# The experts' end of a four-layer kernel: gathers issued together, slot numbers ahead of other work, shared rows added by VectorE, four result and output buffers

## The chip, the cores and the metric

The kernel runs on one core of a Trainium2 chip. The metric is device time in microseconds (us) from the start to the end of one execution; shorter is better. All tensors are float32. TensorE (PE) has two clock levels, 1.2 and 2.4 GHz; the profile gives the granted one as a share of the higher ("PEclk", 0.50 to 1.00).

## What is computed

Eight sequences of 256 rows with 256 columns pass through four residual layers. Each computes `x = x + layernorm(f(layernorm(x)))`. The first three are a state-space mixer with a gated feed-forward, a low-rank mixture of 8 experts, and causal attention. The fourth, where the change lies, is a mixture of 64 experts. In the reference, cut to what matters:

```python
logits = flat @ router_w.T                      # flat: 2048 x 256
_, topk_idx = top_k(logits + router_bias, 4)
topk_w = softmax(logits) at topk_idx, divided by its sum
tok_table = rows of each expert, at most 32     # 64 x 32
xg = flat[tok_table]
g, u = xg @ gate_w, xg @ up_w                   # 256 -> 64, per expert
y = (silu(g) * u) @ down_w                      # 64 -> 256, per expert
out = scatter_add(y * weight) + shared experts(flat)   # 256 -> 512 -> 256
```

## The kernel before

The 2,048 rows are worked on in four rounds of 512, each with four tiles of 128 rows. A round takes its rows through the first three layers. The router, the shared experts and the table of slots of round r-1 are worked in between the first two layers of round r; those of the last round (`LAST` = 3) come behind it by themselves. Each engine has its own program written out by hand, and the engines wait for each other by semaphores. A `BankPlan` gives each PSUM bank its order of users; a user waits until the one before has been read out.

**The last round's router part.** On PE the order is: turn the first half of the normed rows `xf` (`transposes`), `route(0)` (logits of the first half), `project_o(1)` (the attention's last output projection, second half), `shared_hidden(g, 0)` twice (gate and up products of the shared experts for the first half), turn the second half, `route(1)`, `shared_hidden(g, 1)` twice, `shared_down(0)`, `positions` (a running count that gives each choice its place in its expert), `shared_down(1)`, `add_to_table`. On VectorE (DVE): copies of the logits, `routed_experts` (the top four), `routed_counts` (who chose what, for `positions`), `routed_groups` (first the logits of the chosen, a product over 1,024 columns and a sum; then the group of each expert), `shared_gate` for (0, 1) and (1, 1), `routed_slots` (needs `positions`), `routed_places` (first two small operations that release the exponential on ScalarE through `top_ready`; then a 2,048-column comparison, `oh_place`), and `add_rows`, which adds PE's table to the one in SBUF. `result_rows` makes two index tables out of it: `tidx` (which row of `xn_dram` each of the 2,048 slots takes) and `yidx` (to which row of `y_dram` its result goes).

ScalarE (ACT) copies each half of `shared_down` to `tmp` (`shared_sum`), takes the exponential (`expert_exp`), then goes to its part of the experts. SyncE (SP) stores `tmp` into `sh_dram` (`store_shared`), and then loads for all 16 tiles of the output the shared sum and the residual row (`shx[i][:, 0, :]` and `shx[i][:, 1, :]`, 32 transfers of 128 KB) into buffers that by then are free.

**The experts.** The 64 experts are 16 groups of four, worked in eight pairs `p`. The weights are in SBUF. GpSimd (POOL) issues an indirect DMA for each group: `gather(g)` brings 128 rows from `xn_dram` into one of eight buffers `xg`, `scatter(g)` writes 128 result rows from `yt` to `y_dram`. Its order is gathers 0 to 7, then for each pair two scatters and (for the first four) two gathers, into the buffers of the first eight. PE's order for a pair is `turn` (transposes of the gathered rows, bank XG), `gate_up` (32 instructions into 32-column parts of the array, bank GU), `turn_hidden` (HT) and `down` (16 instructions, two banks YO). `turn(p+1)` and `gate_up(p+1)` are issued before `down(p)`. ACT copies XG and HT to SBUF and takes the silu; DVE multiplies (`gate`) and copies YO to `yt` (`results`), of which there are two pairs: `results(p)` waits until the scatters of pair p-2 have landed (`y_out`).

**The sums.** When all scatters have landed, ACT loads tile after tile the four result rows of each of its 128 rows (`yk`, four buffers of 512 KB, queue of ACT). For each of the 16 tiles PE adds in one bank the shared sum (a product with the identity, L570) and the four rows, each by a diagonal matrix of weights (L575). DVE takes mean and variance from the bank (L716, L718, L719), POOL the power (L655), and DVE, one tile behind (`finish`), scales the bank's rows (L708) and adds the residual (L711) into `ot`. There are two `ot`: `finish(i)` waits until the store of tile i-2 has landed (`stored`). SP stores.

Of the kernel before, what the change touches and what calls it, by code (L numbers as in the profile page):

```python
# [107 lines left out]
def sandwich(nc, A, out):  # L108
    with ExitStack() as ctx:
# [334 lines left out]
        xg = [(xin, hn)[s // 4][:, s % 4, :] for s in range(8)]  # L444
# [5 lines left out]
        yt = [u[:, 2 * i:2 * i + 2, :] for i in range(2)]  # L450
# [5 lines left out]
        acc = [tmp[:, s, :] for s in range(2)]  # L456
        ot = [tmp[:, 2 + s, :] for s in range(2)]
# [14 lines left out]
        xg_in = [sem(f"xg_in{s}") for s in range(8)]  # L472
        e_silu = signal("e_silu", EPAIRS)
        y_out = [sem(f"y_out{s}") for s in range(2)]
# [7 lines left out]
        stored = [sem(f"stored{s}") for s in range(2)]  # L482
        chain2 = signal("dve_chain2", 2 * TOKENS // P)
# [15 lines left out]
        def tail_sync(sp):  # L499
            sp.wait_ge(tidx_ready, 1)  # L500
            sp.wait_ge(x3_out, 16 * ROUNDS + CREDIT)
# [5 lines left out]
            for i in range(TOKENS // P):  # L507
                sp.wait_ge(out_ready.sem, i + 1)
                sp.dma_start(out[i * P:(i + 1) * P, :], ot[i % 2]).then_inc(stored[i % 2], 16)
            for s in range(2):  # L510
                sp.wait_ge(stored[s], 16 * (TOKENS // P // 2) + CREDIT)

        def tail_tensor(pe):
            def turn(p):
                for g in (2 * p, 2 * p + 1):
                    pe.wait_ge(xg_in[g % 8], 16 * (g // 8) + 16)
                pe.wait_ge(*tail.before(("XG", p), 0))
                for i in range(2):
                    for k in range(DC):
                        o = (i * DC + k) * P  # L520
                        mm = pe.transpose(tail[("XG", p)][:, o:o + P], xg[(2 * p + i) % 8][:, k * P:(k + 1) * P],
# [43 lines left out]
            for i in range(TOKENS // P):  # L565
# [3 lines left out]
                pe.wait_ge(shx_in[i // 4], 128)  # L569
                mm = pe.matmul(sums[("SUM", i)][:, 0:D], ident[:, :], shx[i][:, 0, :], start=True, stop=False)  # L570
# [3 lines left out]
                for k in range(TOPK):  # L574
                    mm = pe.matmul(sums[("SUM", i)][:, 0:D], diag[i % 2][:, k, :], yk[s][:, k, :],  # L575
                                   start=False, stop=k == TOPK - 1)
                mm.then_inc(sums.fills(("SUM", i)), 1)

        def tail_scalar(act):
# [33 lines left out]
            for s in range(2):  # L613
                act.wait_ge(y_out[s], 16 * EGROUPS // 2)
# [10 lines left out]
        def tail_pool(pool):  # L625
            def gather(g):
                if g >= 8:
                    pool.wait_ge(*tail.full(("XG", g // 2 - 4), 0))
                pool.indirect_dma_start(
                    out=xg[g % 8], out_offset=None, in_=xn_dram,  # L630
                    in_offset=bass.IndirectOffsetOnAxis(ap=tidx[:, g:g + 1], axis=0)).then_inc(xg_in[g % 8], 16)

            def scatter(g):
# [3 lines left out]
                    in_=yt[g // 2 % 2][:, g % 2, :], in_offset=None, bounds_check=TOKENS * TOPK - 1,  # L637
# [1575 lines left out]
```

## Time and profile before

| what | value |
|---|---|
| median of 3 runs | 1291.43 us (1290.85 to 1294.38) |
| profiled execution | 1297.54 us, its span 1295.5 us |
| busy: PE, DVE, ACT, POOL | 1110.3, 867.8, 499.0, 251.8 us |
| instructions | 19826 |
| mean granted PE clock | 0.939 |
| moved by DMA | 111.75 MB |

The span is the time between the first and the last instruction of the profiled execution. The median is of other executions, and is 6.1 us under the profiled one. Times in the views below count from the span's start; the part that the change touches begins at about 1149 us.

### The profile page before, as it was taken

What the parts mean: (1) busy time and instruction counts of PE and PEld (TensorE: products, weight loads), DVE (VectorE), ACT (ScalarE), POOL (GpSimd) and SP (SyncE); (2) the same over time, 40 slices, a digit from 0 to 9 for tenths busy, and PEclk for the clock granted to TensorE, in tenths of its full rate; (3) what the DMA queues carried; (4) which work ended last, traced back from release to release, by engine and by line L of the source; (5) the groups of instructions that cost most, each with busy time, mean ns of one, the idle gap of its engine ahead of it and who ended that gap; (6) DMA issues with size and microseconds to landing.
All of it is one profiled execution on the core that took longest, in us unless ns stands there. A gap on an engine that the chain in (4) does not pass through costs nothing.

```text
span 1295.5 us, 19826 instructions
## 1 busy us (share of the span) xinstructions
PE 1110.3 (86%) x7192; PEld 672.5 (52%) x7192; DVE 867.8 (67%) x1848; ACT 499.0 (39%) x1076; POOL 251.8 (19%) x522
## 2 busy tenths in 40 slices
PE   3999896888998997888998997888998997886667
PEld 1444554554445675554445674554445675465345
DVE  5899526669997545669996636769997546565126
ACT  2766411236665202246665102236664111221133
POOL 3222001132221000222221000222221000222432
PEclk9999998899999997899999997899999997897679
DMA  5888100004431000004331000004348030035345
GB/s 177 284 266 282 36 1 16 1 2 133 120 116 59 1 8 26 2 2 146 121 120 41 1 17 17 1 5 155 122 123 216 4 94 21 2 81 167 118 162 186
DMA packets 72673, 111.75 MB, mean 86 GB/s; under 512 B 5896, under 2 KB 62608, under 8 KB 71682
## 3 DMA queue, kind: packets, MB, share of 16 engines
q1 hardware_dynamic: 68738, 98.51, 24.4%
q10 hardware_dynamic: 2304, 8.39, 2.0%
q0 software_dynamic: 1536, 3.60, 0.9%
q8 instruction: 57, 0.93, 0.3%
q14 instruction: 38, 0.31, 0.1%
HBM read 91.81 MB, written 19.27 MB: 86 GB/s over the span
## 4 chain that ended last, share of the span: by engine, by line
PE 61%; DVE 20%; issue 7%; ACT 6%; DMA 2%; another core or an unknown queue 1%; POOL 1%; DVEq 0%; SPq 0%; POOLq 0%; ACTq 0%
PE bank L883 22%; DVE hf L1651 5%; PE bank L948 4%; PE bank L1124 4%; PE bank L1165 3%; PE bank L1032 3%; PE bank L1048 2%; DVE nmax L2041 2%; PE bank L962 2%; PE bank L1211 2%; DVE u L1871 2%; PE bank L1208 2%; PE bank L896 2%; DMA out_dram<-tmp 2%
## 5 line engine op out<-in xcount | busy, mean ns | idle before, releaser
L883 PE MATMUL bank<-uT,w_in 128*128 128x512 f32 (+1 forms) x584 | 288.2, 621 | 25.0 <-DVE hf L1651 11.3
L1651 DVE SCALAR_TENSOR_TENSOR hf<-bank,conv_w,hf 128x510 f32<-128x510 f32 (+2 forms) x384 | 277.9, 743 | 18.5 <-ACT hf L1366 13.3
L883 PEld LDWEIGHTS bank<-uT,w_in 128*128 128x128 f32 (+1 forms) x584 | 99.9, 188 | 123.3 <-issue 90.1
L1366 ACT ACTIVATE hf<-bank,conv_b,conv_w 128x512 f32<-128x512 f32 x128 | 99.4, 777 | 136.6 <-PE bank L883 136.6
L1493 POOL TENSOR_TENSOR rs<-ve,half 128x2 f32<-128x2 f32 x56 | 39.0, 697 | 382.1 <-DVE ve L1783 382.1
L1032 PE MATMUL bank<-hf 64*128 64x256 f32 x512 | 89.7, 426 | 12.6 <-issue 7.2
L883 PE MATMUL bank<-uT,w_gu 128*128 128x512 f32 x224 | 99.0, 593 | 0.0
L2041 DVE TENSOR_REDUCE nmax<-bank 128x2 f32<-128x256 f32 (+1 forms) x128 | 65.4, 554 | 44.1 <-PE bank L1211 44.1
L1032 PEld LDWEIGHTS bank<-hf 64*128 64x128 f32 x512 | 38.8, 184 | 69.8 <-issue 63.5
L1871 DVE TENSOR_TENSOR turned_p<-dec,bank 128x768 f32<-128x768 f32 x64 | 60.9, 952 | 15.9 <-PE bank L1033 5.0
L1346 ACT ACTIVATE xc<-bank 128x512 f32<-128x512 f32 x44 | 26.3, 597 | 115.3 <-PE bank L883 77.1
L883 PEld LDWEIGHTS bank<-uT,w_gu 128*128 128x128 f32 x224 | 42.3, 190 | 46.6 <-issue 45.9
L1901 DVE TENSOR_TENSOR hf<-xc,bank 128x512 f32<-128x512 f32 x32 | 22.0, 687 | 62.8 <-PE bank L883 44.6
L1124 PE MATMUL bank<-w_dn,hf 128*128 128x256 f32 x256 | 56.2, 380 | 3.6 <-issue 3.6
L948 PE MATMUL bank<-uT_moe,w_sgu 128*128 128x256 f32 x256 | 58.7, 384 | 0.0
L874 PE MATMUL bank<-ident,u 128*128 128x128 f32 x128 | 23.9, 318 | 39.6 <-DVE u L1607 17.1
L948 PEld LDWEIGHTS bank<-uT_moe,w_sgu 128*128 128x128 f32 x256 | 49.6, 194 | 12.1 <-issue 5.7
L1124 PEld LDWEIGHTS bank<-w_dn,hf 128*128 128x128 f32 x256 | 48.3, 190 | 13.2 <-issue 6.8
L1033 PEld LDWEIGHTS bank<-hf 64*128 64x128 f32 x512 | 50.0, 187 | 5.3
L1463 ACT ACTIVATE dec<-bank 128x768 f32<-128x768 f32 x32 | 26.0, 811 | 64.2 <-PE bank L1222 64.2
L1463 ACT ACTIVATE turned_p<-bank 128x768 f32<-128x768 f32 x24 | 19.5, 811 | 80.6 <-PE bank L1222 80.6
L1033 PE MATMUL bank<-hf 64*128 64x128 f32 x512 | 49.9, 270 | 0.0
(314 smaller groups left out, 2174.9 us busy)
## 6 DMA issues: line engine op xcount, KB each, us to landing
hf<-cum_dram SPq DMA_DIRECT2D x32, 384.0 KB, 3.7
dec<-cum_dram SPq DMA_DIRECT2D x32, 384.0 KB, 3.6
tmp<-cum_dram SPq DMA_DIRECT2D x32, 384.0 KB, 3.6
x<-cum_dram SPq DMA_DIRECT2D x32, 384.0 KB, 3.5
y_dram<-xf SPq DMA_DIRECT2D x16, 512.0 KB
hf<-y_dram ACTq DMA_DIRECT2D x16, 512.0 KB, 4.5
w_in<-in_w_in SPq DMA_DIRECT2D x1, 3584.0 KB, 12.0
w_in<-in_w_egu SPq DMA_DIRECT2D x6, 512.0 KB, 9.2
```

The costliest lines, as they stand in the source:

```text
L883: mm = pe.matmul(plan[key][0:n, :], w[:, k, cols], uT[:, k, :], start=k == 0, stop=k == DC - 1)
L948: mm = pe.matmul(plan.of(key, d)[:, i * HALF:(i + 1) * HALF], w_sgu[:, k, o + i * P:o + (i + 1) * P], uT_moe[:, k, j * HALF:(j + 1) * HALF ...
L1032: pe.matmul(cb[:, e, 0:SEQ], B[:, o:o + P], C[:, o:o + SEQ], start=True, stop=True)
L1033: return lambda: pe.matmul(cb[:, e, SEQ:TRI], B[:, o + P:o + SEQ], C[:, o + P:o + SEQ], start=True, stop=True)
L1124: mm = pe.matmul(plan[("F", j)][:, i * D:(i + 1) * D], hf[:, f, t * P:(t + 1) * P], w_dn[:, f, :], start=f == 0, stop=f == FF // P - 1)
L1165: mm = pe.matmul(plan[key][:, cols], w_att[:, k, n, c * P:(c + 1) * P], uT[:, k, cols], start=k == 0, stop=k == DC - 1)
L1366: act.activation(dst, plan[key][:, :], ACT.Identity, bias=conv_b[:, j:j + 1], scale=conv_w[:, j, TAPS - 1:TAPS]).then_inc(tap0.sem, 1)
L1463: act.activation(prT[k % 6], pair_banks(("ST", k))[:, :, 0:TRI], ACT.Exp)\
L1493: pool.tensor_tensor(rs[:, cols], ve[:, cols], half[:, cols], ALU.pow).then_inc(rstd_ready.sem, 1)
L1651: ins = dve.scalar_tensor_tensor(d, x, conv_w[:, j, TAPS - 1 - s:TAPS - s], d, ALU.mult, ALU.add)
L1871: dve.tensor_tensor(sc[g % 4], dec[:, d:d + 2, :], both_cb[g % 2][:, :, 0:TRI], ALU.mult).then_inc(plan.drains(("CB", p, b)), 1)
L2041: ins = dve.tensor_reduce(nmax[:, n // 4 % 2, i, col:col + 33:32], S[:, :, cols], AX.X, ALU.max, negate=True)
```

## The change

The gathers have 16 buffers (`xin`, `hn`, `xf`, `x1`) and are all issued before the first scatter. `yt` has four pairs of buffers in place of two. On PE, `project_o(1)` goes ahead of `route(0)`, `positions` ahead of `shared_down(0)`, and `add_to_table` ahead of `shared_down(1)`. On DVE the two `shared_gate` of the second half, the logits of the chosen (`routed_chosen_logits`) and the two small operations (`routed_top`) go behind `result_rows`. SP's `tail_sync` waits for `top_ready` as well. In the sums, PE's product with the identity is gone; DVE adds the shared rows to the bank, into `acc` in SBUF, and takes its statistics and the scaling from there. `ot` and `acc` have four buffers each. In the earlier rounds the split functions are called one after the other, in the order of before. The diff, cut to its core:

```diff
-        xg = [(xin, hn)[s // 4][:, s % 4, :] for s in range(8)]
+        xg = [(xin, hn, xf, x1)[g // 4][:, g % 4, :] for g in range(EGROUPS)]
...
-        yt = [u[:, 2 * i:2 * i + 2, :] for i in range(2)]
+        yt = [u[:, 2 * i:2 * i + 2, :] for i in range(2)] \
+            + [uT_moe[:, i, :].rearrange("p (g d) -> p g d", g=2) for i in range(2)]
...
-        acc = [tmp[:, s, :] for s in range(2)]
-        ot = [tmp[:, 2 + s, :] for s in range(2)]
+        acc = [xin[:, s, :] for s in range(4)]
+        ot = [tmp[:, s, :] for s in range(4)]
...
         def tail_sync(sp):
             sp.wait_ge(tidx_ready, 1)
+            sp.wait_ge(top_ready.sem, top_ready.at(LAST, 1))
             sp.wait_ge(x3_out, 16 * ROUNDS + CREDIT)
             sp.wait_ge(sh_out, 16 * ROUNDS + CREDIT)
             for i in range(TOKENS // P):
...
                 sp.wait_ge(out_ready.sem, i + 1)
-                sp.dma_start(out[i * P:(i + 1) * P, :], ot[i % 2]).then_inc(stored[i % 2], 16)
-            for s in range(2):
-                sp.wait_ge(stored[s], 16 * (TOKENS // P // 2) + CREDIT)
+                sp.dma_start(out[i * P:(i + 1) * P, :], ot[i % 4]).then_inc(stored[i % 4], 16)
+            for s in range(4):
+                sp.wait_ge(stored[s], 16 * (TOKENS // P // 4) + CREDIT)
...
-                pe.wait_ge(shx_in[i // 4], 128)
-                mm = pe.matmul(sums[("SUM", i)][:, 0:D], ident[:, :], shx[i][:, 0, :], start=True, stop=False)
...
                 for k in range(TOPK):
                     mm = pe.matmul(sums[("SUM", i)][:, 0:D], diag[i % 2][:, k, :], yk[s][:, k, :],
-                                   start=False, stop=k == TOPK - 1)
+                                   start=k == 0, stop=k == TOPK - 1)
...
             def gather(g):
-                if g >= 8:
-                    pool.wait_ge(*tail.full(("XG", g // 2 - 4), 0))
+                if g == 12:
+                    pool.wait_ge(x3_out, 16 * ROUNDS + CREDIT)
                 pool.indirect_dma_start(
-                    out=xg[g % 8], out_offset=None, in_=xn_dram,
-                    in_offset=bass.IndirectOffsetOnAxis(ap=tidx[:, g:g + 1], axis=0)).then_inc(xg_in[g % 8], 16)
+                    out=xg[g], out_offset=None, in_=xn_dram,
...
             pool.wait_ge(tidx_ready, 1)
-            for g in range(8):
+            for g in range(EGROUPS):
                 gather(g)
             pool.wait_ge(yidx_ready, 1)
-            for p in range(EPAIRS):
-                for g in (2 * p, 2 * p + 1):
-                    scatter(g)
-                if 2 * p + 8 < EGROUPS:
-                    for g in (2 * p + 8, 2 * p + 9):
-                        gather(g)
+            for g in range(EGROUPS):
+                scatter(g)
...
             def results(p):
-                if p >= 2:
-                    dve.wait_ge(y_out[p % 2], 32 * (p // 2))
+                if p >= 4:
+                    dve.wait_ge(y_out[p % 4], 32 * (p // 4))
                 for i in range(2):
                     key = ("YO", 2 * p + i)
                     dve.wait_ge(*tail.full(key, 0))
-                    dve.tensor_copy(yt[p % 2][:, i, :], tail[key][:, 0:D]).then_inc(tail.drains(key), 1)
+                    dve.tensor_copy(yt[p % 4][:, i, :], tail[key][:, 0:D]).then_inc(tail.drains(key), 1)
 
             result_rows()
+            for g in range(2):
+                shared_gate(g, 1, g, LAST)
+            routed_chosen_logits(LAST)
+            routed_top(LAST)
             routed_weights(LAST)
             gate(0)
...
             def finish(i):
                 s = i % TILES
                 dve.wait_ge(rstd2.sem, i + 1)
-                dve.wait_ge(stored[i % 2], CREDIT + 16 * (i // 2))
-                a = acc[i % 2]
-                dve.tensor_scalar(a, sums[("SUM", i)][:, 0:D], mv[:, s, 0:1], rs[:, s:s + 1], ALU.subtract,
-                                  ALU.mult).then_inc(sums.drains(("SUM", i)), 1)
-                dve.wait_ge(*sums.drained(("SUM", i), 0))
-                dve.tensor_tensor(ot[i % 2], shx[i][:, 1, :], a, ALU.add).then_inc(out_ready.sem, 1)
+                dve.wait_ge(stored[i % 4], CREDIT + 16 * (i // 4))
+                a = acc[s]
+                link(dve.tensor_scalar(a, a, mv[:, s, 0:1], rs[:, s:s + 1], ALU.subtract, ALU.mult))
+                dve.tensor_tensor(ot[i % 4], shx[i][:, 1, :], a, ALU.add).then_inc(out_ready.sem, 1)
 
             for i in range(TOKENS // P):
                 s = i % TILES
+                dve.wait_ge(shx_in[i // 4], 128)
                 dve.wait_ge(*sums.full(("SUM", i), 0))
-                link(dve.bn_stats(stats[:, s, :], sums[("SUM", i)][:, 0:D]))
+                dve.tensor_tensor(acc[s], sums[("SUM", i)][:, 0:D], shx[i][:, 0, :], ALU.add)\
+                    .then_inc(sums.drains(("SUM", i)), 1)
+                dve.wait_ge(*sums.drained(("SUM", i), 0))
+                link(dve.bn_stats(stats[:, s, :], acc[s]))
                 settle(dve)
                 link(dve.bn_aggr(mv[:, s, :], stats[:, s, :]))
                 dve.tensor_scalar(ve[:, s:s + 1], mv[:, s, 1:2], EPS, None, ALU.add).then_inc(var2.sem, 1)
...
                     linear(pe, ("X", 1), w_in, x_cols[1], r + 1)
+            project_o(1)
             route(0, LAST)
-            project_o(1)
             for g in range(2):
                 shared_hidden(g, 0, LAST)
             transposes(pe, "moe", 4, xf, 1, LAST)
             route(1, LAST)
             for g in range(2):
                 shared_hidden(g, 1, LAST)
+            positions(LAST)
             shared_down(0, LAST)
-            positions(LAST)
+            add_to_table(LAST)
             shared_down(1, LAST)
-            add_to_table(LAST)
             tail_tensor(pe)
...
-            def routed_groups(d):
+            def routed_chosen_logits(d):
                 link(dve.tensor_tensor(prod, oh, lgt[:, :, :].unsqueeze(2).broadcast_to([P, TILES, TOPK, E1]),
                                        ALU.mult))
                 link(dve.tensor_reduce(lk[:, :, :], prod, AX.X, ALU.add))
+
+            def routed_groups(d):
...
-            def routed_places(d):
+            def routed_top(d):
                 link(dve.tensor_reduce(wsum_moe[:, :], lk[:, :, :], AX.X, ALU.max))
                 dve.tensor_tensor(lk[:, :, :], lk[:, :, :],
                                   wsum_moe[:, :].unsqueeze(2).broadcast_to([P, TILES, TOPK]),
                                   ALU.subtract).then_inc(top_ready.sem, 1)
+
+            def routed_places(d):
...
             routed_experts(LAST)
             routed_counts(LAST)
             routed_groups(LAST)
-            shared_gate(0, 1, 0, LAST)
-            shared_gate(1, 1, 1, LAST)
             routed_slots(LAST)
             routed_places(LAST)
             add_rows(LAST)
-            tail_vector(dve, routed_weights)
+            tail_vector(dve, shared_gate, routed_chosen_logits, routed_top, routed_weights)
```

## Rows read from the trace of the kernel before

**Rows 1.** Windows by stage: length; PE, PEld, DVE, ACT, POOL busy (instructions); PEclk; DMA share, GB/s.
```profile
1150.00:1185.50 35.50, 29.73 (x148) 25.19 (x148) 25.32 (x67) 6.88 (x10) 2.85 (x5) 0.90 0.47 134
1185.50:1194.40 8.90, 1.09 (x4) 0.72 (x4) 0.83 (x6) 0.62 (x2) 6.00 (x7) 0.50 0.79 233
1194.40:1242.00 47.60, 30.42 (x422) 17.79 (x422) 8.35 (x24) 11.56 (x32) 23.94 (x25) 0.68 0.36 116
1249.00:1295.50 46.50, 37.50 (x158) 31.16 (x158) 26.01 (x80) 17.89 (x56) 8.84 (x16) 0.94 0.64 208
```
**Rows 2.** Timeline of router part: start, us, engine, line, operation, count, idle before and releaser.
```profile
1150.04 1.08 PE L937 MATMUL bank<-w_rt,uT_moe 128*128 128x64 f32 x8 [0.78 <-ACT uT_moe L1322]
1151.03 3.65 PE L1267 MATMUL bank<-w_att,hf 128*128 128x256 f32 x8
1161.70 0.69 DVE L1683 TENSOR_TENSOR dec<-xc,bank 128x512 f32<-128x512 f32 x1 [0.39 <-PE bank L948]
...
1166.05 8.18 PE L948 MATMUL bank<-uT_moe,w_sgu 128*128 128x256 f32 x32
1174.07 3.62 PE L962 MATMUL bank<-w_sdn,dec 128*128 128x256 f32 x16
1177.95 1.22 DVE L1735 TENSOR_TENSOR sz<-turned_p,bank 128x1024 f32<-128x1024 f32 x1 [0.25 <-PE bank L972]
...
1181.52 0.17 DVE L1751 TENSOR_REDUCE wsum_moe<-lk 128x4 f32<-128x16 f32 x1
1181.81 2.28 DVE L1755 TENSOR_TENSOR yg<-place,iota 128x2048 bf16<-128x2048 f32 x1
```
**Rows 3.** Timeline from the table to the first pair of expert groups, same columns.
```profile
1181.54 0.60 ACT L1352 ACTIVATE tmp<-bank 128x512 f32<-128x512 f32 x1 [3.22 <-PE bank L962]
1182.15 1.28 ACT L1357 ACT_TABLE_LOAD   x1
...
1186.57 1.23 POOL L629 DMA_INDIRECT xin<-xn_dram,tidx  x1 [8.22 <-DVE tidx L669]
1188.11 0.96 POOL L629 DMA_INDIRECT xin<-xn_dram,tidx  x1 [0.30 <-issue]
...
1192.64 1.09 PE L521 MATMUL bank<-ident,xin 128*128 128x128 f32 x4 [7.84 <-issue]
1194.41 1.96 PE L533 MATMUL bank<-w_in,uT 128*32 128x128 f32 x32 [0.69 <-issue]
```
**Rows 4.** Windows from one pair's first DVE result copy (L686) to the next's, columns of Rows 1.
```profile
1202.27:1209.30 7.03, 3.56 (x58) 2.16 (x58) 1.04 (x3) 1.04 (x3) 4.00 (x4) 0.99 0.45 146
1209.30:1215.52 6.22, 4.37 (x53) 2.59 (x53) 1.05 (x3) 1.04 (x3) 4.00 (x4) 0.50 0.22 73
...
1229.48:1233.99 4.51, 3.58 (x52) 2.11 (x52) 0.96 (x4) 1.25 (x4) 2.02 (x2) 0.62 0.20 70
1233.99:1238.12 4.13, 2.25 (x50) 1.31 (x50) 1.04 (x5) 0.94 (x3) 1.97 (x2) 1.00 0.10 35
```
**Rows 5.** Timeline of the sums, PE, then DVE, columns of Rows 2.
```profile
1248.97 3.75 PE L575 MATMUL bank<-hf,h 128*128 128x256 f32 x8 [8.33 <-DMA hf<-y_dram]
...
1279.76 1.89 PE L575 MATMUL bank<-hf,h 128*128 128x256 f32 x8
1281.48 0.59 PE L570 MATMUL bank<-w_sgu,ident 128*128 128x256 f32 x2
...
1288.65 0.42 DVE L716 BATCH_NORM_STATS2 stats<-bank 128x6 f32<-128x256 f32 x1
...
1289.53 0.54 DVE L708 TENSOR_SCALAR tmp<-bank,mv,rs 128x256 f32<-128x256 f32 x1
1290.10 0.43 DVE L711 TENSOR_TENSOR tmp<-w_sgu,tmp 128x256 f32<-128x256 f32 x1
1290.45 0.42 DVE L716 BATCH_NORM_STATS2 stats<-bank 128x6 f32<-128x256 f32 x1
```
**Rows 6.** Waits of 1257 to 1296 us: who waited for whom, total us, times, longest.
```profile
DVE tmp L708 <- DMA out_dram<-tmp: 8.9, 4, 2.8
```

More of the change, by code:

```diff
@@ L471, in sandwich @@
         e_in = [sem(f"e_in{p}") for p in range(EPAIRS)]
-        xg_in = [sem(f"xg_in{s}") for s in range(8)]
+        xg_in = [sem(f"xg_in{g}") for g in range(EGROUPS)]
         e_silu = signal("e_silu", EPAIRS)
-        y_out = [sem(f"y_out{s}") for s in range(2)]
+        y_out = [sem(f"y_out{s}") for s in range(4)]
         tidx_ready = sem("tidx_ready")
@@ L481, in sandwich @@
         out_ready = signal("out_ready", TOKENS // P)
-        stored = [sem(f"stored{s}") for s in range(2)]
-        chain2 = signal("dve_chain2", 2 * TOKENS // P)
+        stored = [sem(f"stored{s}") for s in range(4)]
+        chain2 = signal("dve_chain2", 3 * TOKENS // P)
         diag = [h1[:, 2 * i:2 * i + 2, :].rearrange("p t (k q) -> p (t k) q", q=P) for i in range(2)]
@@ L515, in turn @@
                 for g in (2 * p, 2 * p + 1):
-                    pe.wait_ge(xg_in[g % 8], 16 * (g // 8) + 16)
+                    pe.wait_ge(xg_in[g], 16)
                 pe.wait_ge(*tail.before(("XG", p), 0))
@@ L520, in turn @@
                         o = (i * DC + k) * P
-                        mm = pe.transpose(tail[("XG", p)][:, o:o + P], xg[(2 * p + i) % 8][:, k * P:(k + 1) * P],
+                        mm = pe.transpose(tail[("XG", p)][:, o:o + P], xg[2 * p + i][:, k * P:(k + 1) * P],
                                           ident[:, :])
@@ L612, in tail_scalar @@
             diagonals(1)
-            for s in range(2):
-                act.wait_ge(y_out[s], 16 * EGROUPS // 2)
+            for s in range(4):
+                act.wait_ge(y_out[s], 16 * EGROUPS // 4)
             for s in range(TILES):
@@ L626, in gather @@
             def gather(g):
-                if g >= 8:
-                    pool.wait_ge(*tail.full(("XG", g // 2 - 4), 0))
+                if g == 12:
+                    pool.wait_ge(x3_out, 16 * ROUNDS + CREDIT)
                 pool.indirect_dma_start(
-                    out=xg[g % 8], out_offset=None, in_=xn_dram,
-                    in_offset=bass.IndirectOffsetOnAxis(ap=tidx[:, g:g + 1], axis=0)).then_inc(xg_in[g % 8], 16)
+                    out=xg[g], out_offset=None, in_=xn_dram,
+                    in_offset=bass.IndirectOffsetOnAxis(ap=tidx[:, g:g + 1], axis=0)).then_inc(xg_in[g], 16)
             def scatter(g):
@@ L636, in scatter @@
                     out=y_dram, out_offset=bass.IndirectOffsetOnAxis(ap=yidx[:, g:g + 1], axis=0),
-                    in_=yt[g // 2 % 2][:, g % 2, :], in_offset=None, bounds_check=TOKENS * TOPK - 1,
-                    oob_is_err=False).then_inc(y_out[g // 2 % 2], 16)
+                    in_=yt[g // 2 % 4][:, g % 2, :], in_offset=None, bounds_check=TOKENS * TOPK - 1,
+                    oob_is_err=False).then_inc(y_out[g // 2 % 4], 16)
             pool.wait_ge(xn_out, 16 * ROUNDS + CREDIT)
@@ L656, in tail_pool, with tail_vector @@
                     .then_inc(rstd2.sem, 1)
-        def tail_vector(dve, routed_weights):
+        def tail_vector(dve, shared_gate, routed_chosen_logits, routed_top, routed_weights):
             def result_rows():
@@ L1915, in _ @@
                     if r > 0 and i == 3:
+                        routed_chosen_logits(r - 1)
                         routed_groups(r - 1)
@@ L1919, in _ @@
                     if r > 0 and i == 8:
+                        routed_top(r - 1)
                         routed_places(r - 1)
```

## Prediction, made before the result was known

> **What bounds the kernel now.** I read four views in this order. First the windows by stage over the end of the kernel [rows 1], to see which stretches the change can touch and which engine fills them. In the router part PE is busy for 29.7 of 35.5 us and DVE for 25.3; nothing is idle for long, so the order on both engines counts. Then comes a hole of 8.9 us with 1.1 us of PE work, at half clock. In the experts' loop, 47.6 us, no engine is full: PE shows 30.4 us, POOL 23.9. In the sums, 46.5 us, PE has 37.5 and DVE 26.0.
>
> Second, the timeline of the router part [rows 2]. `project_o(1)` (L1267) runs behind `route(0)` (L937), then `shared_hidden` (L948), and DVE's second shared gate (L1683) stood idle 0.39 us for it: PE sets this stretch. Later `positions` sits behind the sixteen matmuls of `shared_down(0)` (L962), and `routed_slots` (L1735) starts only at 1177.95, 3.7 us after the last `shared_hidden` ended (1166.05 + 8.18 = 1174.23). The reader is to see a chain: L1735, L1755, table, first gather.
>
> Third, the way from the table to the experts [rows 3]. L1755 ends at 1184.09, the first gather is issued 2.48 us later, the second ends its issue at 1189.07, and PE can turn the first pair only at 1192.64, 3.6 us after that, since both must have landed. POOL issues one every 1.26 us.
>
> Fourth, windows cut from one pair's result copy to the next [rows 4]. This is the view that my sum hangs on. Six periods lie between pair 0 at 1202.27 and pair 6 at 1238.12. The four in which POOL issues four indirect DMAs last 6.2 to 7.0 us (two of them shown), the two in which it issues two last 4.1 and 4.5. PE's work is the same, some 50 instructions, and PE's busy time in the 7.03 us is half of it. The clock doesn't sort them: 7.03 us came at 0.99, 6.22 at 0.50. So PE's results come late about as long as POOL is issuing.
>
> Last the sums [rows 5, 6]. DVE needs 1.80 us a tile when nothing holds it (1288.65 to 1290.45), but the fifteen steps from the first bank (1248.97 + 3.75 = 1252.72) to the last L716 (1290.45) take 37.7 us, 2.51 each. Four waits for a store, 8.9 us in sum, stand in between.
>
> **The change part by part.** *Order in the router.* `route(0)` now lies between `project_o(1)` and `shared_hidden`: +1.08 us on PE's path, since `project_o(1)` began only when its data came. Bounds: 0 if DVE's 0.39 us hole and clock luck take it, 2.2 at half clock. `positions` goes ahead of `shared_down(0)`. It can start at 1174.23 + 1.08 = 1175.3, so L1735 starts near 1175.6 in place of 1177.95. DVE is there in time: a product like L1735 (1.22), a sum of the same size and two gates like L1683 (0.69) have left its way, 3.8 us. That is -2.35 with the 1.08 in it. `routed_top` leaves the way too: 1181.81 - 1181.52 = -0.29. `add_to_table` finds PE free either way. L1755 starts at 1179.2, and the first gather at 1183.9 (-2.6).
>
> *What was put behind.* The two gates run after the index tables. I put the tables some 0.9 us before the first gather (an estimate: two thirds of the 2.48 us are left for table and small operations), and 2 x 0.69 behind them the gates end, near 1184.6. They release `shared_down(1)`, which PE now does in what was the hole. Sixteen such matmuls took 3.62 us, eight took 3.65 at the lower clock in L1267: 3.6 to 7.3 us. PE has done little just before, and the old hole was at half clock [rows 1], so I take 5.6: end at 1190.2. The first two gathers (issued by 1186.4) have landed by then; their 3.6 us shrinks if anything, since the 32 `shx` loads, which began beside them, now wait for `sh_dram`. These are 4 MB, 13 to 18 us at the 233 to 325 GB/s that [rows 1] bear out, and nobody needs them before the sums. Queued behind `shared_down(1)`: ACT's copy 0.60, its table load 1.28, the exponential (about 0.2, an estimate from L1751). So ACT turns to the first pair at 1192.3, and `gate_up(0)` starts 0.68 later (1194.41 - 1192.64 - 1.09), near 1193.0 in place of 1194.41: -1.4, between -3.4 and +0.3. Most of the 2.6 us won on the table is lost here. SP waits longer for `top_ready`, which covers nothing else. The chosen logits (2.5 us) lie in DVE's wait for the first silu.
>
> *Sixteen gathers first.* The last is issued at 1183.9 + 1.54 + 14 x 1.26 = 1203.1. The first scatter can't come before 1204.1. Nobody waits for it: `results` now waits from pair 4 on only. While POOL issues, PE is slow, so pair 0 won't gain: I put its copy at 1204.4 (bounds 1200.9, the old one less 1.4, and 1206). From there on every period has two issues. The two rows of that kind are 4.13 and 4.51; I take 4.6, as the first periods have a small queue of scatters and perhaps the lower clock. Pair 6 comes at 1204.4 + 6 x 4.6 = 1232.0 in place of 1238.12: -6.1. Bounds: 6 x 4.2 from 1203.5 gives -9.4. For the other end I count issues beside the loop: before, ten gathers and fourteen scatters, after, nine and fourteen. If each costs the same wherever it lies, the loop gains 1.4 + 1.2 = 2.6. The extra buffers as such bring nothing, since no wait of DVE for a scatter stands in these periods.
>
> The Trainium skill ("SBUF — State Buffer", section "Who interferes with whom") says that only DVE and GpSimd share ports and that PE never waits on anyone. That speaks against my reading of [rows 4]: the long periods would then have another cause, and moving the gathers would not shorten them. It is the third rival below. The sum goes by the rows.
>
> *The sums.* PE drops L570: eight instructions, 1.72 us a tile (1281.48 - 1279.76), less than DVE needs. DVE adds an operation from bank and SBUF: no row has this shape; L711 (both in SBUF) took 0.43, L1683 with twice the columns 0.69. I take 0.43 and 0.03 between. The scaling from SBUF in place of the bank: L708's 0.54 at most, L711's 0.43 nearest, -0.12. So 1.80 + 0.46 - 0.12 = 2.14 us a tile, between 2.05 and 2.35. With four `ot` a store has some 7 us to land, and no wait seen was above 2.8 [rows 6], so I take these waits as gone. Fifteen steps take 32.1 in place of 37.7, -5.6; the first tile's add costs 0.46, and I leave 0.5 for stores and loads that come closer together: 640 KB in 2.14 us is 306 GB/s, against 208 at a share of 0.64, or 325 at full share [rows 1]. That is -4.6, between -6.0 and -1.5. The add that left PE is thus what DVE pays, 5 us of the 8.9 that the stores gave.
>
> *The sum.* -6.1 - 4.6 = -10.7 us. The profiled execution would go from 1297.54 to 1286.8 (span 1284.8); from the median of 1291.43 it is **1280.7**. The earlier rounds run the same instructions.
>
> **The rivals.** (1) As forecast, chance 0.58, 1276 to 1285.
>
> (2) An issue of POOL costs PE the same in the burst as in the loop (the count above): -2.6 - 4.6 gives 1284.2. For it: the burst lies beside `gate_up(0)` and pair 1. Against: the two-issue periods are so short. Chance 0.12.
>
> (3) The long periods aren't POOL's doing and stay near 6.8 us: 1200.9 + 40.8 = 1241.7, +3.6 - 4.6 = -1.0, 1290.4. Against it stand the two short rows. Chance 0.08.
>
> (4) The sums keep 2.5 us a tile, because stores and loads get in each other's way: -6.1, 1285.3. Chance 0.12; with (2) as well, -2.6, 1288.8, chance 0.05.
>
> (5) Slower: the clock falls in the sums. PE was busy 0.81 of that stretch at 0.94; with L570 gone it is 1.72 of 2.14, or 0.80, in shorter pieces. At the lower level eight instructions take 3.75 us [rows 5], 1.6 more than DVE's 2.14. From nine tiles at that level on it eats the forecast and 0.3% (1.6 x 9 = 14.4), with all fifteen the kernel takes 1304. Chance 0.05. The Trainium skill ("TensorE: Matmul & The Clock Gate", "HAM oscillation") warns of just this for a PE that waits between small groups of matmuls.
>
> **How the numbers follow.** A measurement here can tell 0.3%, 3.9 us. Faster by more: (1), (2) and (4) alone, 0.82, of which I move 0.01 to the edge. Within: (3) and (4) with (2), 0.13. Slower: (5), 0.06 with the edge. The bounds of both terms of (1) give -15.4 at the lower end, 1276; I go to 1274 as no bound covers a better clock. Above, 1289 takes in (2) and both forms of (4). Outside lie (3) and (5).
>
> **What would show it.** L1735 near 1175.6; the first gather near 1183.9, sixteen in one row of POOL; `gate_up(0)` near 1193; six periods of 4.2 to 5.0 us; L716 to L716 2.1 us with no wait for stores. It would be wrong if the periods keep 6 us though POOL issues only two, if `shared_down(1)` with ACT's table load makes `gate_up(0)` later than 1194.4, or if DVE's tile takes over 2.4.

## The result

Eight times of the two kernels, four each: after 1272.93 us median (1271.62 to 1275.86), before 1291.14 (1285.72 to 1294.38). The ratio is 0.9866, 95% interval 0.9828 to 0.9905. The direction was forecast. The size was not: -18.2 us in place of -10.7, and 1.1 us below the low end of the range.

### The profile page after: what moved, and what is told of

It is laid out like the page before. It is cut to its first block, busy times and chain, and to the rows that moved or that the text cites. A ratio compares the mean times of both kernels' runs of the same rounds, so it can differ in the third digit from the quotient of the medians.

```text
span 1269.9 us, 19777 instructions
## 1 busy us (share of the span) xinstructions
PE 1089.1 (86%) x7140; PEld 662.3 (52%) x7160; DVE 871.9 (69%) x1864; ACT 498.6 (39%) x1076; POOL 252.8 (20%) x522
## 4 chain that ended last, share of the span: by engine, by line
PE 59%; DVE 22%; issue 9%; ACT 6%; POOL 3%; DMA 1%; DVEq 0%; POOLq 0%; SPq 0%; ACTq 0%
PE bank L885 23%; DVE hf L1653 5%; PE bank L1126 4%; PE bank L950 4%; PE bank L1167 3%; PE bank L1034 3%; DVE nmax L2049 2%; PE bank L1050 2%; DVE u L1877 2%; PE bank L1213 2%; PE bank L1210 2%; PE bank L964 2%; PE bank L898 2%; PE bank L1197 1%; PE bank L1269 1%
## 5 line engine op out<-in xcount | busy, mean ns | idle before, releaser
L1877 DVE TENSOR_TENSOR turned_p<-dec,bank 128x768 f32<-128x768 f32 x64 | 60.9, 952 | 15.9 <-PE bank L1035 5.0
L885 PEld LDWEIGHTS bank<-uT,w_gu 128*128 128x128 f32 x224 | 42.3, 190 | 46.6 <-issue 45.9
L1126 PEld LDWEIGHTS bank<-w_dn,hf 128*128 128x128 f32 x256 | 48.3, 190 | 13.2 <-issue 6.8
L950 PEld LDWEIGHTS bank<-uT_moe,w_sgu 128*128 128x128 f32 x256 | 48.5, 190 | 11.6 <-issue 5.7
L1035 PE MATMUL bank<-hf 64*128 64x128 f32 x512 | 49.9, 270 | 0.0
```

The lines of the kernel that those rows point to most:

```text
L885: mm = pe.matmul(plan[key][0:n, :], w[:, k, cols], uT[:, k, :], start=k == 0, stop=k == DC - 1)
L950: mm = pe.matmul(plan.of(key, d)[:, i * HALF:(i + 1) * HALF], w_sgu[:, k, o + i * P:o + (i + 1) * P], uT_moe[:, k, j * HALF:(j + 1) * HALF ...
L1035: return lambda: pe.matmul(cb[:, e, SEQ:TRI], B[:, o + P:o + SEQ], C[:, o + P:o + SEQ], start=True, stop=True)
L1126: mm = pe.matmul(plan[("F", j)][:, i * D:(i + 1) * D], hf[:, f, t * P:(t + 1) * P], w_dn[:, f, :], start=f == 0, stop=f == FF // P - 1)
L1877: dve.tensor_tensor(sc[g % 4], dec[:, d:d + 2, :], both_cb[g % 2][:, :, 0:TRI], ALU.mult).then_inc(plan.drains(("CB", p, b)), 1)
```

## The profile after

The profiled execution of after has a span of 1269.9 us and a mean granted clock of 0.948. First the timeline on the way to the experts (start, duration, engine, line; in brackets the idle time ahead of it and what ended it). L1739 here is L1735 of [rows 2], L1761 is L1755, L1359 is L1352 of [rows 3], L535 is L533.

```profile
1174.46 1.21 DVE L1739 TENSOR_TENSOR sz<-turned_p,bank 128x1024 f32<-128x1024 f32 x1
1178.09 2.29 DVE L1761 TENSOR_TENSOR yg<-place,iota 128x2048 bf16<-128x2048 f32 x1
1182.86 1.23 POOL L629 DMA_INDIRECT xin<-xn_dram,tidx  x1 [6.48 <-DVE tidx L665]
...
1190.57 1.28 ACT L1359 ACT_TABLE_LOAD   x1
...
1192.62 0.68 PE L535 MATMUL bank<-w_in,uT 128*32 128x128 f32 x8 [2.27 <-ACT uT L582]
```

`routed_slots` starts at 1174.46 (forecast 1175.6), the first gather at 1182.86 (1183.9), `gate_up(0)` at 1192.62 (1193.0). The execution is 0.31 us later than that of before when it enters this part (`project_o(1)` at 1151.34, in before at 1151.03 [rows 2]), so counted from there the gather comes 1.4 us earlier than forecast, 4.0 us earlier than in before. The reason is in the second `route` and the last `shared_hidden`. First before, then after:

```profile
1164.53 1.73 PE L937 MATMUL bank<-w_rt,uT_moe 128*128 128x64 f32 x8 [0.78 <-ACT uT_moe L1322]
1166.05 8.18 PE L948 MATMUL bank<-uT_moe,w_sgu 128*128 128x256 f32 x32
...
1151.34 3.63 PE L1269 MATMUL bank<-w_att,hf 128*128 128x256 f32 x8 [1.77 <-issue]
...
1165.73 1.08 PE L939 MATMUL bank<-w_rt,uT_moe 128*128 128x64 f32 x8 [0.78 <-ACT uT_moe L1324]
1166.64 7.12 PE L950 MATMUL bank<-uT_moe,w_sgu 128*128 128x256 f32 x32
```

They take 1.7 us less at a granted clock of 1.00 (1165.7 to 1173.8) than in before at 0.82 (1164.5 to 1174.2), which more than pays for the 1.08 us of the first `route`.

Next, windows cut from one pair's result copy to the next, as in [rows 4].

```profile
1198.10:1201.10 3.00, 2.42 (x54) 1.57 (x54) 1.06 (x4) 1.04 (x3) 2.30 (x3) 1.00 0.97 268
1207.08:1210.56 3.48, 2.90 (x58) 1.93 (x57) 1.05 (x4) 1.04 (x3) 2.84 (x3) 1.00 1.06 367
1210.56:1213.13 2.57, 1.99 (x52) 1.27 (x51) 1.04 (x4) 1.04 (x3) 1.96 (x3) 1.00 0.97 325
```

A pair takes 3.0 us, not the 4.6 that I had taken, and it does so at full clock while POOL issues without a pause. The seven periods are 2.99, 2.99, 2.98, 3.48, 2.57, 2.98 and 1.72. The 3.48 holds a wait of DVE of 0.49 us for a scatter, and the next period is shorter for it; the last pair has no pair behind it. So PE is *not* late while POOL issues, and the step on which my sum hung is wrong. What sets the end is seen in POOL's timeline, and in all of POOL's waits of this stretch (total, times, longest).

```profile
1182.86 1.23 POOL L629 DMA_INDIRECT xin<-xn_dram,tidx  x1 [6.48 <-DVE tidx L665]
...
1201.94 0.95 POOL L629 DMA_INDIRECT x<-xn_dram,tidx  x1 [0.30 <-issue]
1203.19 1.02 POOL L635 DMA_INDIRECT y_dram<-u,yidx  x1 [0.30 <-issue]
...
1222.59 0.98 POOL L635 DMA_INDIRECT y_dram<-uT_moe,yidx  x1 [0.31 <-issue]
1225.12 1.79 ACTq L496 DMA_DIRECT2D hf<-y_dram  x4
```

```profile
POOL y_dram L635 <- issue: 4.9, 16, 0.3
POOL x L629 <- issue: 1.2, 4, 0.3
POOL hn L629 <- issue: 1.2, 4, 0.3
POOL xf L629 <- issue: 1.2, 4, 0.3
POOL xin L629 <- issue: 0.9, 3, 0.3
```

POOL waits for nobody. Thirty-two issues run from 1182.86 to 1223.57, 40.7 us, 1.27 each. The last copy of results starts at 1217.83, and four scatters are still to be issued. The load of the result rows follows the last scatter's landing. It comes 20.5 us earlier than in the profiled execution of before:

```profile
1245.64 1.79 ACTq L495 DMA_DIRECT2D hf<-y_dram  x4
```

The sums: DVE in one tile (L718 is L716 of [rows 5], L709 is L711), and DVE's one large wait there, which is that for the first tile.

```profile
1236.81 0.42 DVE L715 TENSOR_TENSOR xin<-bank,dec 128x256 f32<-128x256 f32 x1
1237.26 0.43 DVE L718 BATCH_NORM_STATS2 stats<-xin 128x6 f32<-128x256 f32 x1
1237.83 0.18 DVE L720 BATCH_NORM_AGGREGATE mv<-stats 128x2 f32<-128x6 f32 x1
1238.05 0.15 DVE L721 TENSOR_SCALAR ve<-mv 128x1 f32<-128x1 f32 x1
1238.13 0.41 DVE L708 TENSOR_SCALAR xin<-xin,mv,rs 128x256 f32<-128x256 f32 x1
1238.58 0.42 DVE L709 TENSOR_TENSOR tmp<-dec,xin 128x256 f32<-128x256 f32 x1
1238.92 0.42 DVE L715 TENSOR_TENSOR xin<-bank,dec 128x256 f32<-128x256 f32 x1
1239.37 0.43 DVE L718 BATCH_NORM_STATS2 stats<-xin 128x6 f32<-128x256 f32 x1
```

```profile
DVE xin L715 <- PE bank L575: 14.7, 2, 13.7
```

A tile takes 2.11 us (2.14 forecast), DVE has 2.01 us of work in it, and the waits for a store are gone.

## The experiments

All kernels give five numbers from one trace: the start of `project_o(1)`, of the first gather and of the first load of results, the time between the last two (the loop), and the time from that load to the end of the span (the sums). In brackets behind a ratio stands its 95% interval. The medians of one block share a chip, where before had 1290.28 (e1 to e4), 1289.16 (e5 to e8) and 1290.45 us (e9 to e12). After was measured on another one.

| kernel | median us (runs), ratio to before | `project_o(1)` | gather | load | loop | sums |
|---|---|---|---|---|---|---|
| before | see above | 1151.03 | 1186.57 | 1245.64 | 59.1 | 49.9 |
| after | 1272.93 (4), 0.9866 | 1151.34 | 1182.86 | 1225.12 | 42.3 | 44.8 |
| e1_gathers_first | 1282.93 (10), 0.9952 [0.9935, 0.9970] | 1151.02 | 1186.57 | 1230.37 | 43.8 | 48.1 |
| e2_sums | 1286.86 (12), 0.9970 [0.9955, 0.9986] | 1156.13 | 1191.67 | 1242.38 | 50.7 | 45.0 |
| e3_router | 1285.69 (12), 0.9973 [0.9956, 0.9989] | 1151.60 | 1183.10 | 1233.31 | 50.2 | 50.5 |
| e4_interleaved | 1283.64 (8), 0.9953 [0.9936, 0.9971] | 1153.66 | 1185.17 | 1237.27 | 52.1 | 45.0 |
| e5_before_again | 1285.05 (1) | 1151.44 | 1186.97 | 1237.20 | 50.2 | 45.8 |
| e6_four_results | 1288.83 (10), 1.0001 [0.9984, 1.0018] | 1153.05 | 1188.59 | 1238.68 | 50.1 | 46.8 |
| e7_two_results | 1277.74 (6), 0.9895 [0.9874, 0.9917] | 1151.42 | 1182.92 | 1231.00 | 48.1 | 44.9 |
| e8_add_on_pool | 1269.63 (5), 0.9835 [0.9813, 0.9857] | 1152.98 | 1184.49 | 1226.78 | 42.3 | 41.9 |
| e9_before_3_spare | 1289.93 (10), 0.9998 [0.9982, 1.0015] | 1150.23 | 1185.77 | 1236.54 | 50.8 | 48.7 |
| e10_after_4_spare | 1276.02 (4), 0.9875 [0.9855, 0.9894] | 1155.56 | 1187.06 | 1234.32 | 47.3 | 44.2 |
| e11_after_again | 1274.97 (4), 0.9872 [0.9851, 0.9893] | 1153.51 | 1185.02 | 1227.28 | 42.3 | 44.7 |
| e12_pool_adds_again | 1268.63 (5), 0.9827 [0.9805, 0.9850] | 1155.18 | 1186.68 | 1228.93 | 42.2 | 41.9 |

**The parts alone, and the whole without one.** e1 is before with 16 gather buffers and this order on POOL:

```diff
-            for g in range(8):
+            for g in range(EGROUPS):
                 gather(g)
...
-            for p in range(EPAIRS):
-                for g in (2 * p, 2 * p + 1):
-                    scatter(g)
-                if 2 * p + 8 < EGROUPS:
-                    for g in (2 * p + 8, 2 * p + 9):
-                        gather(g)
+            for g in range(EGROUPS):
+                scatter(g)
```

> The kernel before with one part of the change: sixteen gather buffers and all gathers issued ahead of the scatters; router order, result buffers and sums as before. Theory A (gathers issued between the scatters make PE's completions late): pair-to-pair periods fall from 6.2-7.0 us to about 3.0 us and 8 to 14 us are won. Theory B (any issue of POOL makes PE late, as predicted): periods of 4 to 5 us, 2 to 6 us won. Theory C (the late completions belong to some other state of PE, such as its clock, and only happened in the one profiled execution of before): periods don't depend on the order, gain under 3 us.

e2 is before with DVE's addition of the shared rows and four `ot`; e3 is before with the order of the router.

> The kernel before with the sums of the change alone: DVE adds the shared rows, four output buffers; nothing else. Predicted for this part: 2.14 us a tile, -4.6 us (between -6.0 and -1.5). The profiles of the full change show 2.11 us a tile and 44.8 us from the first load to the end in place of 49.9. If the parts add up, 4 to 5.5 us are won. The experts' periods should look as in before: if they don't (under 5 us), the late completions are not a property of the order of issues.

> The kernel before with the router part of the change alone (PE's order, gates and logits of the chosen behind the index tables, SP's added wait). Predicted: the table 2.6 us earlier, gate_up of pair 0 only 1.4 us earlier (the full change showed 1.8). If the parts add up, 0.5 to 2.5 us are won. Rival: the loads of the shared rows no longer lie beside the first gathers, which shortens the loop too: 3 us or more.

e4 is after with this order taken back, so eight buffers and gathers between the scatters.

> The full change with one part undone: eight gather buffers, gathers between the scatters as in before (each also waits for PE's transposes of the pair four before it). Theory A: periods return to 6-7 us, the time goes back by 8 to 14 us, to 1281-1287. Theory B: the number of issues beside the loop is nearly the same, so little changes, under 3 us. Theory C: no rule in the periods, under 3 us on the median.

Each part alone is faster: -7.4, -3.4, -4.6 us, -15.4 in sum. Against before on its own chip e4 keeps 6.6 us, so it has lost 11.6 of the -18.2, of which 9.8 are in the loop. Some expectations were missed: e1 has periods near those of theory A (2.4 to 3.5 us, but for one of 7.52) and less than its 8 us; e2 brings less than 4; and e3 more than 2.5, though not by the way of its rival, since its loop is no shorter than that of the other kernels with the old order on POOL. What no theory had expected stands in the loop of e2 and e3. The order of before gives 50.7 and 50.2 us there, not 59.1. Its first two periods are short (2.99 and 3.33, 2.98 and 3.77 us) though POOL's order is that of before, and then come long ones, up to 9.33 us in e4. That long period of e4, in PE's timeline:

```profile
1205.64 0.66 PE L552 MATMUL bank<-w_in,w_lora 64*32 64x256 f32 x16
1211.09 1.08 PE L523 MATMUL bank<-ident,xin 128*128 128x128 f32 x4 [4.79 <-issue]
```

PE has nothing for 4.79 us until it turns pair 4, whose gathers POOL issued at 1204.35 and 1205.65, behind the scatters of pair 0. In e1 the one long period (7.52 us) is another wait, DVE's for a scatter to leave the result buffer:

```profile
1210.78 0.76 DVE L682 COPY u<-bank 128x256 f32<-128x256 f32 x2 [4.42 <-DMA y_dram<-u,yidx]
```

**Does PE's lateness come back?** e5 is before, unchanged.

> The kernel before, unchanged, profiled once more. In its first profiled execution the first gather is at 1186.57 and the first load of result rows at 1245.64, 59.1 us apart, and 29 of PE's completions came 1.3 to 4.0 us after the ends of their matmuls. Theory B (the prediction's: POOL's issuing makes PE's completions late) expects the same again: more than 20 late completions and 57 to 60 us from the first gather to the load. Theory W (PE is not slowed by POOL; a period of PE's and ScalarE's own work is 3.0 us, and the long periods are waits for a gather or a scatter to land; the late completions belong to that one execution) expects at most 3 late completions, one to four periods of 5 to 9 us behind the fourth pair, and 49 to 53 us from the first gather to the load, as in the three runs that keep the interleaved order (50.7, 50.2, 52.1).

No. The loop takes 50.2 us, and the periods are 2.98, 3.06, 6.60, 4.96, 5.73, 5.65 and 1.72. In the first profile of before, the waits of the loop name a releaser that the view can't place, since PE's signals came after the recorded ends of its matmuls:

```profile
ACT w_lora L587 <- remote: 12.4, 4, 4.0
ACT uT L582 <- remote: 8.7, 4, 2.7
DVE u L686 <- remote: 6.9, 5, 2.4
```

In the same stretch of e5, and of all other kernels, there is no such line. In that first profile POOL isn't what bounds a round, and PE doesn't wait for gathers. Each of the four rounds behind the first begins with a wait of POOL for DVE (2.05, 1.31, 2.06 and 2.09 us), and the turn of pair 4 (L521) follows the matmuls ahead of it without a wait for its rows:

```profile
1210.53 1.02 POOL L635 DMA_INDIRECT y_dram<-u,yidx  x1 [2.05 <-DVE u L686]
...
1211.94 1.10 PE L550 MATMUL bank<-w_in,w_lora 64*32 64x256 f32 x16
1212.98 1.11 PE L521 MATMUL bank<-ident,xin 128*128 128x128 f32 x4
```

So the long periods of [rows 4] come with late signals, and are not the ordinary way of this kernel. The execution took 1297.54 us, above all other times of before (1284.9 to 1294.8). POOL, PE and ACT's queue in e5:

```profile
1186.97 1.23 POOL L629 DMA_INDIRECT xin<-xn_dram,tidx  x1 [8.24 <-DVE tidx L669]
...
1196.01 0.94 POOL L629 DMA_INDIRECT hn<-xn_dram,tidx  x1 [0.30 <-issue]
1202.00 1.02 POOL L635 DMA_INDIRECT y_dram<-u,yidx  x1 [5.04 <-DVE u L686]
...
1205.92 0.98 POOL L629 DMA_INDIRECT xin<-xn_dram,tidx  x1 [0.30 <-issue]
...
1208.91 0.63 PE L521 MATMUL bank<-ident,xin 128*128 128x128 f32 x4 [2.33 <-issue]
...
1230.88 0.98 POOL L635 DMA_INDIRECT y_dram<-u,yidx  x1 [3.16 <-DVE u L686]
...
1234.75 0.98 POOL L635 DMA_INDIRECT y_dram<-u,yidx  x1 [0.30 <-issue]
1237.20 0.83 ACTq L495 DMA_DIRECT2D hf<-y_dram  x2
```

From here the ordinary loop can be read. POOL's eight gathers end at 1196.95, the first results are not there yet, and POOL stands idle for 5.04 us. Then each round of two scatters and two gathers takes it 5.2 us, against 3.0 us that PE and ACT need for a pair. So PE waits for gathers that are queued on POOL (2.33 us at 1208.91, 3.0 us after the second gather of pair 4 was issued), and at the end POOL waits for PE, 3.16 us. POOL's stretch is 1235.73 - 1186.97 = 48.8 us, against 40.7 in after: 8.1 us. The two holes are 7.6 of them (5.04 + 3.16, less the 0.30 that lies between any two issues), and the issues themselves the other 0.5. Gathers first fill both holes, since POOL has sixteen issues that need no result.

**What the four result buffers are worth.** e6 is before with `yt` of four pairs, e7 is after with two:

```diff
-        yt = [u[:, 2 * i:2 * i + 2, :] for i in range(2)] \
-            + [uT_moe[:, i, :].rearrange("p (g d) -> p g d", g=2) for i in range(2)]
+        yt = [u[:, 2 * i:2 * i + 2, :] for i in range(2)]
```

> Before, with four pairs of result buffers and nothing else. Theory W: in the interleaved order a pair of results has long left its buffer when the pair after next arrives, since the loop waits for gathers to land; so nothing changes: 1288 to 1291 us here, within 0.3% of before, 49 to 53 us from the first gather to the load. Rival V (the results' buffers hold the loop also in the old order): 2 to 5 us faster, 1285 to 1288.

> After, with two pairs of result buffers as before. Theory W: the scatters come behind all 16 gathers, the first at 20.3 us behind the first gather, and results(2) waits for it to land (2.4 us) before its copy: one period of about 7 us appears (7.5 in the run with the gathers alone, with a wait of 4.4 us). From there two buffers must go round: two scatters issued 2.6, landed 2.4, copied 0.8, 5.8 us for two pairs against POOL's 5.2; over the six pairs left that is 1.5 to 2.5 us. Expected 1274.4 to 1275.5, and 43.8 to 45 us from the first gather to the load against 42.3. Rival (the four result buffers are worth nothing, since POOL issues back to back either way): 1272.9, within 0.5 us of after. Rival (they are worth all of the gain that gathers first has in the full change over alone, some 3 us and more): 1276 to 1279.

Nothing in the old order. With gathers first the loop grows from 42.3 to 48.1 us, more than I had expected (43.8 to 45), and the time was that of the second rival (1276 to 1279):

```profile
1211.30 0.76 DVE L681 COPY u<-bank 128x256 f32<-128x256 f32 x2 [7.17 <-DMA y_dram<-u,yidx]
```

The first scatters, issued at 1203.27 and 1204.59 behind sixteen gathers, kept this copy until 1211.30; I had put 2.4 us for a landing. PE then stands still, so POOL does too, 7.1 us in four waits. In e1 the same wait was 4.42 us and the loop 43.8, though its scatters too stand behind sixteen gathers. The two differ in how busy the DMA engines are. The router's new order also moves SP's 32 loads of shared and residual rows: the first is issued at 1194.13 in after and at 1185.67 in before, and in e7 the last at 1211.29, beside the scatters. In the table, "time" runs from the issue of the second of two indirect DMAs to the instruction that waited for it:

| kernel | router's order | waited for | time, us | DMA share meanwhile |
|---|---|---|---|---|
| e5 | old | gathers of pair 4 | 2.99 | 0.36 |
| e3 | new | gathers of pair 4 | 5.68 | 0.93 |
| e4 | new | gathers of pair 4 | 5.44 | 0.96 |
| e1 | old | scatters of pair 0 | 2.59 | 0.29 |
| after | new | scatters of pair 0 | 6.04 | 1.06 |
| e7 | new | scatters of pair 0 | 6.71 | 1.05 |

So the order on POOL decides when the scatters are issued, and the landing takes the longer the fuller the DMA engines are; e3 is before with the router's order alone, so there it is this order that doubles the landing. That it does so by SP's loads is read from the shares, and no run moves the loads alone. So three parts of the change meet here: gathers first make the scatters late, the loads make them later, and four buffers make late scatters harmless.

**Is POOL the bound?** Spare gathers of rows already gathered, into a buffer that nobody reads: three behind the eighth gather of before (e9), four behind the sixteenth of after (e10).

```diff
+            for g in range(4):
+                pool.indirect_dma_start(
+                    out=hf[:, g, 0:D], out_offset=None, in_=xn_dram,
+                    in_offset=bass.IndirectOffsetOnAxis(ap=tidx[:, g:g + 1], axis=0)).then_inc(spare_in, 16)
```

> Before, with three gathers more behind the first eight, of rows already gathered, into a buffer that nobody reads. Theory I (POOL's issues are the loop's bound, and what the old order loses is the time in which POOL stands idle): in the second profile of before POOL is idle for 5.04 us between its eighth gather and the first scatter, and 3 issues of 1.29 us, 3.9 us, fit in; they cost nothing: 50 to 51.5 us from the first gather to the load of results, 1288 to 1291 us. Rival B (each issue costs, since PE's results come late while POOL issues): 2 to 4 us slower.

> After, with four gathers more between the sixteenth gather and the first scatter, of rows already gathered, into a buffer that nobody reads before the load of results. Theory I: POOL has no idle time in the loop of after, so each costs its 1.28 us: 42.3 + 5.1 = 47.4 us from the first gather to the load of results, and 1277.5 to 1279 us against 1272.9. Rival (PE and ScalarE, at 3.0 us a pair, bound the loop, and POOL follows): less than 1 us slower.

In e9 the hole shrinks from 5.04 to 1.35 us, and the loop is that of the other kernels with the old order (50.8 us; their mean is 50.7):

```profile
1198.56 0.95 POOL L636 DMA_INDIRECT xf<-xn_dram,tidx  x1 [0.30 <-issue]
1200.85 1.02 POOL L642 DMA_INDIRECT y_dram<-u,yidx  x1 [1.35 <-DVE u L695]
```

In e10 the loop grows by 5.0 us, from 42.3 in e11 to 47.3, as forecast (5.1). The medians don't show it, 1276.02 against 1274.97, and 1277.5 at least had been expected. By the granted clock listed with each run, three of the four runs of e10 had 0.948 (1275.1 to 1276.1 us) and one 0.944 (1280.25, the profiled one); all four of e11 had 0.943 to 0.945 (1273.8 to 1276.3), and two of after's 0.948 (1271.6 and 1272.0). At the like clock the spare gathers cost 3.2 to 6.5 us (the runs of after are from another chip). So the trace bears the theory out, and the median of four runs is too coarse for it.

**Is DVE the bound in the sums?** e8 is after with the last addition on POOL; e11 and e12 are after and e8 side by side.

```diff
-                dve.tensor_tensor(ot[i % 4], shx[i][:, 1, :], a, ALU.add).then_inc(out_ready.sem, 1)
...
+            def total(i):
+                pool.wait_ge(scaled.sem, i + 1)
+                pool.wait_ge(stored[i % 4], CREDIT + 16 * (i // 4))
+                pool.tensor_tensor(ot[i % 4], shx[i][:, 1, :], acc[i % 4], ALU.add).then_inc(out_ready.sem, 1)
```

> After, with the last addition of a tile (the residual rows) on POOL in place of DVE. In the profile of after DVE has 2.01 us of work in a tile of 2.11 us (0.42, 0.43, 0.18, 0.15, 0.41, 0.42), and PE's eight products take 1.89. Theory D (DVE is what bounds the sums of after): DVE's work falls to 1.6 us, PE becomes the bound with 1.9 us, 16 tiles by 0.2 gives 3 us: 1269.5 to 1271, a tile in 1.85 to 1.95 us. Rival P (POOL's addition of 256 columns costs above 1.3 us beside its power of 0.67, or slows DVE's instructions beside it): a tile in 2.1 us or more, 1273 to 1280.

> After, unchanged, on the same chip as the run that follows: 1272 to 1274 us, a tile of the sums in 2.1 us.

> The kernel of e8_add_on_pool again, beside after on one chip. Theory D (DVE bounds the sums of after by 2.0 us of work in a tile): 2.4 to 3.3 us below e11_after_again, 1269 to 1271 us. Rival (the difference between e8_add_on_pool and after was that of their chips): within 1 us of it.

Both times the sums take 41.9 us, against 44.7. One tile of e8, 1.73 us from L725 to L725 (11 of the 15 steps have 1.71 to 1.75, four are longer, and the mean is 1.86), and two groups of DVE over the sums (busy, mean ns of one, idle before):

```profile
1246.89 0.42 DVE L725 TENSOR_TENSOR xin<-bank,xc 128x256 f32<-128x256 f32 x1 [0.18 <-issue]
1247.09 0.72 POOL L644 TENSOR_TENSOR tmp<-turned_p,xin 128x256 f32<-128x256 f32 x1
1248.37 0.65 POOL L657 TENSOR_TENSOR rs<-ve,half 128x1 f32<-128x1 f32 x1 [0.56 <-DVE ve L731]
1248.62 0.42 DVE L725 TENSOR_TENSOR xin<-bank,xc 128x256 f32<-128x256 f32 x1
```

```profile
L716 DVE TENSOR_SCALAR xin<-xin,mv,rs 128x256 f32<-128x256 f32 x16 | 6.9, 430 | 0.4 <-POOL rs L657 0.4
L728 DVE BATCH_NORM_STATS2 stats<-xin 128x6 f32<-128x256 f32 x16 | 6.8, 427 | 0.6
```

POOL's addition takes 0.72 us, and with the power it has 1.37 us of work in a tile, below the 1.73. DVE has 1.59 left. I had put PE as the next bound with 1.9; the 1.73 is close to the 1.72 that its eight products take [rows 5], so it is probably PE. Ahead of two of the longer steps PE waits 0.17 and 0.58 us for loaded rows. e12 is 6.3 us below e11 in the medians, more than expected (2.4 to 3.3); at a like clock it is 1272.5 against 1273.8 (0.945) and 1273.6 against 1276.0 (0.944), so 1.3 to 2.4 us, near the 2.8 of the sums in the traces. This version is faster than both kernels.

## Why the prediction was wrong, point by point

- *Order in the router.* Mechanism right, size too small: -2.6 forecast, -4.0 measured. From `project_o(1)` to the first gather the six traces with the old order have 35.53 to 35.55 us, the eight with the new one 31.50 to 31.52. The missed term is the clock. I had let `route(0)` cost 1.08 us on PE's path, between 0 and 2.2; in the new order the second `route` and the last `shared_hidden` run at full clock and take 1.7 us less.
- *"Most of the 2.6 us won on the table is lost here."* Wrong as to the kernel. `gate_up(0)` moved as forecast (1192.62, forecast 1193.0), behind `shared_down(1)` and the table load. But POOL begins with the first gather and bounds the loop from there, so the whole 4.0 us counts.
- *"So PE's results come late about as long as POOL is issuing."* This step failed. In after PE takes 3.0 us a pair beside a POOL that never pauses. In the ordinary old order (e5) POOL is slower than PE, 5.2 us a round against 3.0 a pair, and PE waits for gathers in POOL's queue. [Rows 4] don't even show that: they are of an execution with late signals of PE, whose loop took 59.1 us in place of 50.7 (the mean of e2 to e6 and e9). I took a trait of one trace for a law. The forecast loop was shorter for a wrong reason, and that the direction came out is in part luck.
- *The loop.* -6.1 with the router's share; measured -4.0 and 42.3 - 50.7 = -8.4, so -12.4. Rows of before held the right bound: the second gather's issue ends 2.5 us after the start of the first [rows 3], and 32 issues of some 1.27 us make 40.7 us from the first gather. With that, pair 6 at 1232 was never the question; the last scatter was.
- *"The extra buffers as such bring nothing."* True in the old order (e6), false with gathers first (e7, 5.8 us of loop). I had looked for the wait in the rows of before, where a scatter is issued as soon as its result is copied; the change moves it behind eight more gathers. Nor did I ask what SP's loads, which I had moved later, would then lie beside.
- *The sums.* Mechanism and tile right, 2.11 for 2.14 us. The term was -4.6; over six traces each the sums take 48.3 us in the old form and 44.8 in the new: -3.5. The old form varies from 45.8 to 50.5 and the new only from 44.2 to 45.0.
- *The sum.* -4.0 - 8.4 - 3.5 = -15.9 us. The two comparisons of after with before gave -18.2 and -15.5, and the interval of the first reaches from -12.3 to -22.2. Much of the spread lies ahead of all this: the fourteen traces reach `project_o(1)` between 1150.23 and 1156.13 us.
- *The rivals.* (2), an issue of POOL costs PE the same anywhere: e9 refutes it. (3), the long periods aren't POOL's slowing of PE: its premise was right, its end (6.8 us stay) was wrong. The rule of the Trainium skill beside it ("SBUF — State Buffer", "Who interferes with whom", PE never waits on anyone) agrees with the 3.0 us periods of after. (4) and (5) did not come: the tiles of after have 2.11 us, and the clock is 1.00 from 1236 to 1264 (the mean of the sums, 0.87, comes from their first tiles and their end, where PE had been idle).

Why PE's signals were late in that one execution, and less so where POOL issued two, stays open; it did not occur again, so no run could tell.

## What to carry to other kernels

Before asking why an engine is slow in a loop, multiply out the one that issues: instructions times duration with the gap between them, here 32 x 1.27 = 40.7 us, and compare it with the stretch; the difference is its idle time, and that is what an order can win. When a queue's work is moved ahead, ask what is now behind it and which buffer that holds: more gather buffers paid in full only with more result buffers. When transfers are put off because nobody needs them yet, look at what they will then lie beside. And look at a second execution of the kernel before, or at its times beside the profiled one, ahead of resting a sum on how long one trace took: 1297.54 against a median of 1291.43 was a sign that I only scaled away.

## What the runs showed that I had not expected

- An indirect DMA of 128 rows occupies POOL for 1.27 us with its gap in the mean of the 32 of after, but its landing is far from constant. The last scatter of after landed 2.44 us after its issue, at a DMA share of 0.21 meanwhile. For one DMA of this kind the Trainium skill ("DMA: Bandwidth & Descriptors", "Anatomy of one DMA — SWDGE (gpsimd) path") gives 2.0 us and a term by size, for 128 KB an estimate of 2.3, and here the trace agrees. With the DMA engines at a share of 0.93 to 1.06 the landings that PE or DVE waited for took 5.4 to 6.7 us (e3, e4, e7, e10, after).
- Times of one kernel go with the mean granted clock of the run, whichever causes the other: e12 had 1267.9 to 1268.6 us at 0.949 and 1272.5 and 1273.6 at 0.945 and 0.944. Medians of four or five runs can differ by this alone.
- POOL's addition of 256 columns beside DVE's work (0.72 us, DVE's like instruction 0.42) hardly touched DVE's instructions in the sums: the scaling took 430 ns in the mean against 413 in after, BATCH_NORM_STATS2 427 in both.
